# Graph network on one core: where the next chunk's last five membership tiles are turned in layers 1 to 3

## The reference

```python
xl = (x @ W).reshape(N, H, C)
a_src = jnp.sum(xl * att_src[None], axis=-1)
a_dst = jnp.sum(xl * att_dst[None], axis=-1)
e = jax.nn.leaky_relu(a_src[src] + a_dst[dst], NEG_SLOPE)
m = jax.ops.segment_max(e, dst, num_segments=N)
ex = jnp.exp(e - m[dst])
denom = jax.ops.segment_sum(ex, dst, num_segments=N)
alpha = ex / (denom[dst] + 1e-16)
out = jax.ops.segment_sum(alpha[:, :, None] * xl[src], dst, num_segments=N)
```

## Time and profile before

| what | us |
|---|---|
| median of 3 timed runs | 12305.61 |
| lowest, highest | 12281.99, 12338.94 |
| span of the profiled execution, first to last instruction | 12335.1 |
| PE, DVE, ACT, POOL busy in that span | 7368.8, 5183.6, 2180.5, 6252.3 |

### The profile page before, as it was taken

The page is one execution under the profiler, slowest core; times in us unless marked ns, Lnnn a source line. Parts: engine busy times, 40 slices in busy tenths (PEclk is TensorE's granted clock), DMA queues, the critical chain, the costliest instruction groups (busy, mean ns, idle before and its releaser), DMA issues.

```text
span 12335.1 us, 141293 instructions
## 1 busy us (share of the span) xinstructions
PE 7368.8 (60%) x41611; PEld 6500.9 (53%) x41612; DVE 5183.6 (42%) x13628; ACT 2180.5 (18%) x7255; POOL 6252.3 (51%) x6594
## 2 busy tenths in 40 slices
PE   5666666666565555665565555555555555565554
PEld 5655555555555545554455555554544555555554
DVE  3222222224444444444464444444445444444445
ACT  2111111112111111111121111111112111111112
POOL 4555555554455545554445555555544555555553
PEclk7777777777777777777767777777776777777776
DMA  3222222222211111111122121121112221111111
GB/s 88 55 55 55 55 54 55 56 55 59 51 47 47 47 45 47 47 46 45 46 67 48 47 48 48 48 48 48 47 47 55 49 48 48 48 48 48 48 48 42
DMA packets 425594, 625.69 MB, mean 51 GB/s; under 512 B 189754, under 2 KB 305737, under 8 KB 425285
## 3 DMA queue, kind: packets, MB, share of 16 engines
q0 software_dynamic: 206336, 462.61, 15.4%
q1 hardware_dynamic: 218910, 160.84, 5.0%
q10 hardware_dynamic: 296, 1.65, 0.0%
HBM read 598.03 MB, written 26.58 MB: 51 GB/s over the span
## 4 chain that ended last, share of the span: by engine, by line
another core or an unknown queue 29%; PE 25%; DVE 23%; issue 16%; DVEq 4%; ACT 2%; POOL 1%; DMA 0%; SPq 0%; ACTq 0%; POOLq 0%
PE ps L713 12%; PE ps L760 7%; DVE acc L1263 5%; DVE memb L1183 4%; DVEq L1237 2%; PE ps L703 2%; DVE msg L1356 2%; DVE msg L1276 1%; DVEq L1263 1%; PE ps L791 1%; DVE acc L1253 1%; DVE shared L1310 1%; PE ps L795 1%; DVE shared L1348 1%
## 5 line engine op out<-in xcount | busy, mean ns | idle before, releaser
L568 POOL DMA_INDIRECT G<-rows,idx x6448 | 6112.1, 948 | 5686.5 <-DVE msg L1356 2881.2
L713 PE MATMUL ps<-msg,memb 128*128 128x136 f32 (+2 forms) x12896 | 2052.4, 328 | 62.9 <-DVE msg L1356 62.2
L760 PE MATMUL ps<-membT,shared 128*104 128x128 f32 x9672 | 2082.8, 400 | 2.2 <-ACT membT L925 2.2
L713 PEld LDWEIGHTS ps<-msg,memb 128*128 128x128 f32 x12896 | 1976.0, 236 | 84.0 <-issue 41.1
L760 PEld LDWEIGHTS ps<-membT,shared 128*104 128x104 f32 x9672 | 1874.9, 270 | 29.5 <-issue 3.0
L703 PE MATMUL ps<-ident,memb 128*128 128x128 f32 x6448 | 1108.2, 302 | 1137.5 <-issue 750.3
L1183 DVE TENSOR_TENSOR memb<-rel,ps 128x768 f32<-128x768 f32 x1488 | 1044.4, 729 | 1509.1 <-PE ps L713 1227.7
L703 PEld LDWEIGHTS ps<-ident,memb 128*128 128x128 f32 x6448 | 770.4, 150 | 1393.4 <-issue 1034.4
L925 ACT ACTIVATE membT<-ps 128x512 f32<-128x512 f32 x1984 | 991.3, 510 | 1961.8 <-remote 1639.2
L732 PE MATMUL ps<-shared,membT 128*128 x3224 | 813.8, 336 | 754.2 <-DVE msg L1276 472.5
L1263 DVE TENSOR_TENSOR acc<-acc,ps 128x136 f32 (+2 forms) x3472 | 1023.0, 295 | 561.7 <-issue 315.5
(11 more groups left out here) (182 smaller groups left out, 4864.9 us busy)
## 6 DMA issues: line engine op xcount, KB each, us to landing
G<-rows,idx POOLq DMA_INDIRECT x6448
shared<-marks_all SPq DMA_DIRECT2D x372, 156.0 KB
shared<-in_edge_attr SPq DMA_DIRECT2D x124, 256.0 KB
shared<-in_edge_attr SPq DMA_DIRECT2D x124, 160.0 KB
rows<-msg SPq DMA_DIRECT2D x36, 288.0 KB, 2.7
idx<-in_src SPq DMA_DIRECT2D x496, 6.5 KB
xrows<-msg SPq DMA_DIRECT2D x24, 256.0 KB, 2.2
memb<-xrows SPq DMA_DIRECT2D x24, 256.0 KB, 2.9
```

The source lines that it names most:

```text
L568: nc.gpsimd.indirect_dma_start(G[:, b, t, 0:rows[l].shape[1]], None, rows[l], bass.IndirectOffsetOnAxis(idx[:, b, t:t + 1], 0)).then_inc(g ...
L713: last = mm(ps_sum[k // 2][:, 0:width], memb[:, b, k * P:(k + 1) * P], msg[:, b, k, 0:width], start=k % 2 == 0, stop=k % 2 == 1 or k == K - 1)
L760: last = mm(ps_sc[b][0:JH, :], adz[:, k // 2, K - 1 - k:K - 1 - k + JH], membT[:, k, :], start=k == 0, stop=False)
```

## The change

On PE the third and fourth batch of the next chunk's membership are turned behind the turned weights (L791), right ahead of the second `target_scores`, and no longer between the tile ends and the carries. On ACT both copies now follow the weights' exponential. The same instructions run; no wait is added or removed. The last chunk of a layer and layer 0 are untouched.

```diff
--- before.py
+++ after.py
@@ -773,8 +773,6 @@
                               segm[0:JH, e:e + 1], ident[0:JH, 0:JH].rearrange("p (h k) -> p h k", h=H),
                               start=True, stop=True)
                 last.then_inc(ends_out, 1)
-                if ahead:
-                    turn(l, c + 1, 1 - b, (2, 3))
                 pe.wait_ge(run_kept, gpast(l, c))
                 pe.wait_ge(carry_ready, gpast(l, c))
                 for w in range(2):
@@ -790,6 +788,7 @@
                 pe.wait_ge(wgt_ready, gpast(l, c))
                 nc.tensor.transpose(ps_wgt, wgt[0:JH, :], ident[0:JH, 0:JH]).then_inc(wgt_turned, 1)
                 if ahead:
+                    turn(l, c + 1, 1 - b, (2, 3))
                     target_scores(l, c + 1, 1 - b, 8, K)
                 pe.wait_ge(fac_less, gpast(l, c))
                 mm(ps_fac, memb[0:1, b, 0:P], factor[0:1, 2 * H:4 * H], start=True, stop=True).then_inc(fac_out, 1)
@@ -989,8 +988,6 @@
                     keep_turned(l, c + 1, 1)
                 act.wait_ge(fac_diff, gpast(l, c))
                 nc.scalar.activation(factor[0:1, 2 * H:3 * H], factor[0:1, 2 * H:3 * H], ACT.Exp).then_inc(fac_exp, 1)
-                if ahead:
-                    keep_turned(l, c + 1, 2)
                 if l == 1:
                     act.wait_ge(maxf_turned, gpast(l, c))
                     copy(msg[:, b, :, MW:SW].rearrange("p k h -> p h k"),
@@ -998,6 +995,7 @@
                 act.wait_ge(diff_ready, gpast(l, c))
                 nc.scalar.activation(wgt[0:JH, :], diff[0:JH, :], ACT.Exp).then_inc(wgt_ready, 1)
                 if ahead:
+                    keep_turned(l, c + 1, 2)
                     keep_turned(l, c + 1, 3)
 
             def edges(l, c, b, h, ahead=True):
```

## The result

The changed kernel takes 12,855 us (median of 4 runs, 12,805 to 12,903), the kernel before, in runs beside it, 12,321 us (12,282 to 12,339): ratio 1.044 [1.041, 1.048]. That is slower, as forecast, and inside the range, but it moved by 4.4%, where the forecast was +280 us on 12,305.6, or 2.3%.

What follows compares the result with a forecast made beforehand. PE's signals, late while gathers run, were taken to pin L1337 at 18.4 us after the first gather (usual period 23.8 us). Layer 1 +157 and layers 2 and 3 +123 gave +280 on 12,305.6: 12,585 us, range 12,290 to 12,870.

Steps and rivals of the forecast that it cites:

- Held stretch, passes and pin: PE's signals come late during gathers, 1.05 us per queued pass; L1337 is pinned 18.4 us after the first gather.
- R: Rival in the experiments: late signals are a matter of PE's own queue, so a later start against the gathers costs nothing.
- rival C: Faster: late signals belong to PE's own queue, so five passes fewer ahead of the carries gain 500 us: 11,800; chance 0.08.
- First half of the change worth nothing in usual chunks: Five turns taken from ahead of the carries: L1337 stays at the gathers' end; bounds 0 and 2.4 us a chunk.
- The sums' start: Sums wait for turns, copies and ten passes: 3.3 us after L791's end at full clock, 5.2 at half.
- The start of L767: Behind a half-clock end, L767 moves 1.5 us later after the first gather, from 3.8 to 5.3.
- part of the half-clock delay comes back, as the sums would run at full clock by then: Sums: 7 to 9 of 25 steps slow, 0.1 us each; delay of 2.5 us taken as 1.5 at L767.
- The price in layers 2 and 3: Chunks behind half-clock ends (59%) take 24.6 less 0.3 us, else 23.75: mean 24.1, +0.5 for 246 chunks, +123 us.
- rival A: The clock rises later because PE idles before L760; lengths 26.5 us in layers 2 and 3 too: 12,805 us; chance 0.24.
- Layer 1: Long chunks of 27.6 us at share 0.47, others 23.9: mean 25.6, +1.3 us for 123 chunks, +157 us.
- Full-clock ends: Behind a full-clock end L767 starts 1.1 us later, 4.4 on average, 3.7 after a long chunk; layer 1 length 23.9.

Runs made afterwards that it cites:

- e3: The changed kernel with the ten passes of the second target_scores moved behind the sums: 13,803 us against 12,840 for the kernel before, ratio 1.075.
- e6: The kernel before with the four turns of batch 1 made twice in layers 1 to 3: 12,706 us against 12,303, ratio 1.032.
- e2: The kernel before with the third and fourth batch neither turned nor copied inside the chunks: 12,533 us against 12,840, ratio 0.977.
- e9: The changed kernel with the factor products, made four times, between the turns and the ten passes: 12,904 us against 12,336 for the kernel before, ratio 1.047.
- e4b: The kernel before with rows of layers 1 to 3 fetched by 13 plain SP transfers a chunk, no POOL gathers there: 9,344 us against 12,348, ratio 0.757.

## Why the prediction came out right in sign and too small in size

**Held stretch, passes and pin: right.** Only where the indirect gathers run are PE's signals late; without them all are on time. R and with it rival C are refuted. I had turned the count of passes into a start of L767, since the two go together in the kernel before; e3 (start 3.5 us, scan 18.5) and e6 (same starts, scan 2 to 3 us later) part them, and both count.

**First half of the change worth nothing in usual chunks: about right.** Leaving the turns out altogether gives 0.8 us a chunk (e2). In the changed kernel the usual chunk of layer 1 has its carries' step at 18.4 us still.

**The sums' start: right for the sums.** Forecast 5.2 us behind the turned weights' end at half clock and 3.3 at full, measured 4.7 and 2.9 to 3.1. The wait for ACT's copy is there, 0.80 us each.

**The start of L767: too early behind half-clock ends.** Forecast 5.3 us, measured 6.2, 5.6 and 5.8. The step that failed is "part of the half-clock delay comes back, as the sums would run at full clock by then". They don't: 8.8, 5.4 and 8.4 of their steps are slow behind such an end, where it was 5.8, 7.8 and 7.9 before, because the clock rises later. Behind the turned weights' end it rises in the median after 3.7, 4.2 and 4.7 us before the change, and after 6.9, 5.6 and 6.4 behind it. Part of that is how the chunks are sorted: a chunk whose clock rises ahead of the ten passes now counts as a full-clock end. Of the chunks whose clock is half at the turned weights' end, 43 of 81 in layer 2 and 36 of 75 in layer 3 rise within 2 us, and none of the others before 5 us; before the change it was 9 of 77 and 10 of 76, and most rose after 3 to 5 us. In layer 1 none of 55 rises within 2 us, before or after, and the median goes from 3.8 to 6.9 us. Counted from the first of the ten passes the two kernels differ by +1.3, -0.5 and -0.2 us. The Trainium skill, "TensorE: Matmul & The Clock Gate", section "Part 4: PE-mode transpose", says that transposes don't lead to the full clock. By that rule the turns give nothing toward the rise in their new place, which is what layer 1 shows; the early rises in layers 2 and 3, with only turns behind the turned weights, neither fit it plainly nor refute it, as PE's 16 passes of L760 stand between the carries and the turned weights. What decides when the clock rises here stays open, and that the narrow factor products of e9 didn't help either is part of it.

**The price in layers 2 and 3: the step that made the size wrong.** I took 24.3 us behind a half-clock end there, from 20 chunks of the kernel before with L767 over 5 us and the scan at 15.6. Measured is the scan at 18.4 and 27.2 us. Those 20 chunks had 40 passes between the first gather and the tile ends; the changed kernel has 48 to 49 there, since the rest of the ten passes and the factor's two now run inside the gathers, and L767 comes 0.4 to 0.6 us later still. The forecast's share of such chunks was too high (.59; it is .32 and .39), which gives little back. For layer 2: 0.32 x (27.2 - 24.3) = 0.93 us more from the price, 0.68 x (24.1 - 23.75) = 0.24 from the full-clock ends, and 0.27 x (24.3 - 23.75) = 0.15 less from the share, together +1.0 on a forecast of +0.5. This is the outcome of rival A, which gave 26.5 us, a share of .37 and 12,805 us. The changed kernel took 12,855. Of A's mechanism one part isn't borne out: filling PE's break (e9) didn't bring the rise forward.

**Layer 1: near.** Forecast .47 x 27.6 + .53 x 23.9 = 25.6, measured .51 x 28.0 + .49 x 24.1 = 26.1.

**Full-clock ends: a little dearer.** The start of L767 was forecast at 3.7 to 4.4 and is 3.4 us, yet the scan stands at 13.6, 14.9 and 13.5 in the mean, later than the 12.4 of a usual chunk before. There are 42 to 43 passes instead of 41. The measure left something out here too, and by luck not much.

Of the 286 us that the forecast lacks (572 less the forecast's 1.3 + 0.5 + 0.5 us, times 124), layer 1 has 0.45 x 124 = 56 us, layer 2 0.98 x 124 = 122 and layer 3 0.88 x 124 = 109.

What stays open: what in the chip holds the signals. The runs show that the hold is there with the indirect gathers, that shorter plain transfers from the same queue don't bring it, and how late the signals come, but not through which part they are held, nor the rule by which starts and passes together set the scan. Why the kernel before takes 4% more on one chip is open as well; in the profiles taken there layer 0 has 24.1 us a chunk instead of 23.4, so it isn't the gathers of layers 1 to 3 alone.

## What to carry to other kernels

Where an engine's results reach the others late only while a certain kind of transfer runs, two things are to be looked at: how many instructions that engine makes between the start of the transfers and the result that the others need, and how late in the transfers that result comes; moving work off the path behind such a result helps nothing if it lands ahead of the next one. Moving the start of the transfers behind the tight hand-offs, with one added wait on the transfers' side, and 16 passes out of those hand-offs gave 7.4% here, while moving PE's work into the stretch ahead of them cost 4.4%.

When a relation is read from the chunks of one kernel (late start, late end), it should be asked what else differs between those chunks before it is used for a kernel in which only one of the two moves.

## What the hardware showed that I had not expected

The indirect gathers hold PE's completion signals and plain transfers of the same rows do not: 12,348 us to 9,344 with the rows fetched by SP, 12,303 to 9,406 with POOL, at the same number of transfers and bytes, though the plain ones are issued in 6 to 7 us and the gathers in 16. Under indirect gathers the tile ends' signal came up to 10.4 us behind the record's end in the inner chunks of the kernel before, and 18.4 us after the first gather, with the gathers over, whatever was queued counted as done. The Trainium skill, "SBUF — State Buffer", section "SBUF: two separate sides", says that PE doesn't wait for the others there and that transfers don't slow the engines. For plain transfers the runs agree. For indirect ones PE's own records keep their usual lengths (the tile ends take 0.52 us at full clock in the kernel before and in e4b), so the page isn't contradicted; but those who wait for PE wait for the gathers, so that it can't be used as a rule for the time.

The hold grows with the passes made under the gathers: one turned batch more cost 1.1 us a chunk (0.66 us of work in the records), and five turns 9 us into the gathers, with 22 or 23 passes made since their start, came through on time.
